# Two-layer graph attention on one core: the second layer's scaled rows made tile by tile inside the projection, with a reference per group of tiles

## The reference

```python
# layer 0, N=4096, F=256, 8 heads of 128
Wh = einsum('nf,hfd->hnd', x, W_heads)
e = s1[:, :, None] + s2[:, None, :]            # s1 = Wh.a1, s2 = Wh.a2
e = where(e > 0, e, 0.2 * e); e = where(adj > 0, e, NEG)
hp = elu(einsum('hnm,hmd->hnd', softmax(e), Wh))
x = layernorm(x + feat @ W_out + b_out)        # feat: 4096 x 1024
# layer 1, 4 heads of 64
xt = einsum('ni,hio->hno', x, W)
e = leaky_relu(src[:, :, None] + dst[:, None, :], 0.2), masked by adj
x = layernorm(x + concat_heads(softmax(e) @ xt))
```

## Time and profile before

| | |
|---|---|
| median of 3 runs | 2834.19 us (2832.05 to 2834.41) |
| the profiled execution | 2831.95 us, span 2830.2 us |
| PE, ACT, DVE, POOL busy | 96%, 72%, 69%, 20% of the span |
| mean granted TensorE clock | 0.987 of full speed |
| stages, start of the first instruction | projection 2066.0, last tile's projection done 2244.2, first attention matmul 2305.9, last 2815.2 us |

### The profile page before, as it was taken

The page is one execution under the profiler, slowest core; times in us unless marked ns, Lnnn a source line. Parts: engine busy times, 40 slices in busy tenths (PEclk is TensorE's granted clock), DMA queues, the critical chain, the costliest instruction groups (busy, mean ns, idle before and its releaser), DMA issues.

```text
span 2830.2 us, 62581 instructions
## 1 busy us (share of the span) xinstructions
PE 2714.5 (96%) x26702; PEld 2350.6 (83%) x26702; DVE 1964.6 (69%) x3078; ACT 2049.7 (72%) x3212; POOL 571.4 (20%) x445
## 2 busy tenths in 40 slices
PE   7889999999999999999999999999999959999997
PEld 3438887888888888888888888888888849999997
DVE  5456678777677776776777767765644468888887
ACT  4447886777777777777787877777722279999996
POOL 0030027233223231422332322310001150000000
PEclk9999999999999999999999999999999979999999
DMA  7985431101110110111110101021134253223330
GB/s 257 396 307 178 154 98 48 30 29 34 29 34 22 40 30 26 37 29 30 33 34 25 38 25 34 22 54 44 25 120 142 86 193 107 93 95 107 111 111 16
DMA packets 189144, 235.19 MB, mean 83 GB/s; under 512 B 13594, under 2 KB 113050, under 8 KB 188860
## 3 DMA queue, kind: packets, MB, share of 16 engines
q1 hardware_dynamic: 188868, 231.20, 25.7%
HBM read 180.49 MB, written 50.66 MB: 82 GB/s over the span
## 4 chain that ended last, share of the span: by engine, by line
PE 73%; DVE 4%; ACT 4%; POOL 2%; issue 1%; ACTq 0%; DVEq 0%; POOLq 0%
PE l_ps L660 56%; PE l_ps L748 11%; PE l_ps L697 4%; ACT l_arena L924 3%; PE l_ps L685 1%; DVE l_arena L1263 1%; DVE l_arena L1262 1%; PE l_ps L717 1%; DVE l_arena L1270 1%; POOL l_arena L370 1%; ACT l_arena L936 1%; POOL l_arena L357 0%; PE l_ps L714 0%; DVE l_arena L1290 0%; DVE l_arena L1251 0%
## 5 line engine op out<-in xcount | busy, mean ns | idle before, releaser
L660 PE MATMUL l_ps<-l_arena 128*128 128x258 f16 x16384 | 1833.3, 273 | 7.1 <-POOL l_arena L346 3.4
L660 PEld LDWEIGHTS l_ps<-l_arena 128*128 128x128 fp8e4 x16384 | 1591.7, 97 | 246.4 <-DVE l_arena L1114 4.3
L855 ACT ACTIVATE l_arena<-l_arena 128x512 fp8e4<-128x512 f32 x2048 | 1281.4, 708 | 89.3 <-PE l_ps L660 89.2
L1113 DVE SCALAR_TENSOR_TENSOR l_arena<-l_arena,l_mask 128x512 uint32<-128x512 uint32 x512 | 468.9, 916 | 407.3 <-ACT l_arena L855 404.6
L748 PE MATMUL l_ps<-l_arena 128*128 128x130 f16 x8192 | 491.6, 222 | 42.9 <-DVE l_arena L1263 40.9
L748 PEld LDWEIGHTS l_ps<-l_arena 128*128 128x128 fp8e4 x8192 | 486.6, 98 | 48.1 <-DVE l_arena L1263 46.5
L1114 DVE TENSOR_TENSOR l_arena<-l_arena,l_mask 128x512 uint32<-128x512 uint32 x512 | 489.9, 957 | 0.0
L924 ACT ACTIVATE l_arena<-l_arena 128x1024 fp8e4<-128x1024 f32 x432 | 453.4, 1141 | 1.2 <-PE l_ps L748 1.2
L339 POOL TENSOR_TENSOR l_arena<-l_arena 128x516 f32<-128x516 f32 x120 | 156.9, 1307 | 1263.4 <-PE l_ps L660 1170.4
L873 ACT COPY l_arena<-l_ps 128x258 f32<-128x258 f32 x256 | 93.7, 369 | 243.5 <-PE l_ps L660 243.5
L1119 DVE SCALAR_TENSOR_TENSOR l_arena<-l_ps,l_arena 128x258 f32<-128x258 f32 x256 | 116.9, 481 | 146.4 <-ACT l_arena L873 146.4
(11 more groups left out here) (142 smaller groups left out, 1246.3 us busy)
## 6 DMA issues: line engine op xcount, KB each, us to landing
l_arena<-in_adj SPq DMA_DIRECT2D x128, 512.0 KB, 7.0
l_arena<-uv SPq DMA_DIRECT2D x128, 260.0 KB, 5.3
l_wh<-l_arena SPq DMA_DIRECT2D x64, 256.0 KB, 9.3
l_arena<-l_srow SPq DMA_DIRECT2D x64, 256.0 KB, 3.3
l_arena<-l_wh SPq DMA_DIRECT2D x64, 256.0 KB, 4.7
feat<-l_arena SPq DMA_DIRECT2D x64, 256.0 KB, 2.2
l_arena<-feat SPq DMA_DIRECT2D x32, 512.0 KB, 3.7
uv<-l_arena SPq DMA_DIRECT2D x8, 1040.0 KB, 4.7
```

What stands on the lines that cost most here:

```text
L660: last = nc.tensor.matmul(sums(t, m), pattern(k, m).bitcast(F8)[:, j, t * P:(t + 1) * P], uv[:, slot(h, order[k]) + j, 2 * m * W1:2 * (m + ...
L855: ins = act.activation(pattern(k, 0).bitcast(F8)[:, j, :], s1b[q][:, :], ACT.Relu, bias=kc[:, h, jt:jt + 1], scale=STEEP, saturate=False)
L1113: dve.scalar_tensor_tensor(c, v, ONE8X4, m, ALU.bitwise_xor, ALU.bitwise_and)
```

## The change

It touches layer 1 only. (a) The scores and rows of a tile come from one matmul pair of 264 columns, two tiles after its projection (`rows_tile`); transposed tiles are kept for two tiles only. (b) Each group c of 4 tiles has its own reference, `kall`: its peak, rounded to a whole multiple of 5 ln 2, so that `eu` and `ev` of a group can be made, scaled and stored (`store_stage`) while later tiles are projected. (c) Once all references are known, `kmax` is the largest; a group's rows then need a factor 2^(5d) or 2^d, d = (kall - kmax)/(5 ln 2), which is exact in f16. `rescales` makes the factors and `rescale(h, k)` multiplies a loaded slice, two instructions of 128x4x130. (d) Each head is rescaled once and stored back (`store_back`): head 0 before and in sweep 0 (slices 0 to 5 ahead of it), head 1 in sweep 0 and behind its `divide2`, head 2 in sweep 1, head 3 in sweep 2. (e) `feat` has two buffers instead of four; slices 0 to 2 of sweep 0's patterns are made in the projection.

The pieces stand in the order of the file: POOL, SP, PE, ACT (its order after the loop last), DVE (in the projection's loop, in the sweeps, at sweep 0's end).

```diff
-            for u in range(PAIRS + 1):
-                if u < PAIRS:
-                    scale2(u)
-                if u > 0:
-                    low2(u - 1)
+                if t >= 9 and t % 4 == 1:
+                    scale2((t - 9) // 4)
+                if t >= 10 and t % 4 == 2:
+                    low2((t - 10) // 4)
+            for c in range(CPB - 2, CPB):
+                scale2(c)
+                low2(c)
...
-                sp.dma_start(fin[t % 4], feat[t * P:(t + 1) * P, :]).then_inc(s_fl[t % 4], 16)
+                sp.dma_start(fin[t % 2], feat[t * P:(t + 1) * P, :]).then_inc(s_fl[t % 2], 16)
...
+            for k in range(CPB - 2):
+                load_uv(0, k)
...
+            store_rows(CPB - 2)
+            for k in range(CPB - 2):
+                store_back(0, k)
+            store_rows(CPB - 1)
+            store_stage(CPB - 2)
+            sp.wait_ge(s_us, 16 * (CPB - 1))
+            load_uv(0, CPB - 2)
+            store_stage(CPB - 1)
...
+            def rows_tile(t):
                 pe.wait_ge(s_xt, t + 1)
+                if t > 0:
+                    pe.wait_ge(s_wc, t)
                 for k in range(KF2):
+                    last = nc.tensor.matmul(pw2, xt2[t % 2][:, k, :], wall2[:, k, :], start=(k == 0),
                                             stop=(k == KF2 - 1))
...
+                    if g < FIRST:
+                        pe.wait_ge(s_res, CPB * g + k + 1)
...
+            def exps(c):
+                act.wait_ge(s_tr2, c + 1)
+                act.activation(by_head(eu2, c), by_head(ta2, c), ACT.Exp).then_inc(s_ex2, 1)
+                act.activation(by_head(ev2, c), by_head(ta2, c), ACT.Exp, scale=SLOPE).then_inc(s_ex2, 1)
...
+            def high_u(c):
+                act.wait_ge(s_tu, c + 1)
+                if c > 0:
+                    act.wait_ge(s_us, 16 * c)
+                act.copy(staged(0), heads(tempu).rearrange("p t h e -> p h t e")).then_inc(s_hu, 1)
...
+            copy_row2(NT - 1)
+            copy_turned(CPB - 1)
+            high_u(CPB - 2)
+            high_v(CPB - 2)
+            compare2(0, 3, range(JC2))
+            exps(CPB - 1)
+            compare2(0, 4, range(JC2))
+            high_u(CPB - 1)
+            high_v(CPB - 1)
+            row_factors()
...
+                ch.link(dve.tensor_scalar(kall[:, c, :], kt, ROUND, ROUND, ALU.add, ALU.subtract))
...
+            def rescale(h, k):
+                q, c = h % 2, SWEEP[h % 2][k]
+                part2 = uv2[:, q, c * JC2 * W4:(c + 1) * JC2 * W4].rearrange("p (t w) -> p t w", t=JC2)
+                dve.wait_ge(s_uv2[q][k], 16 * (h // 2 + 1))
+                dve.tensor_scalar(part2[:, :, 0:2 * V1], part2[:, :, 0:2 * V1], fu.bitcast(F32)[:, c, h:h + 1], None,
+                                  ALU.mult)
+                dve.tensor_scalar(part2[:, :, 2 * V1:], part2[:, :, 2 * V1:], fv.bitcast(F32)[:, c, h:h + 1], None,
+                                  ALU.mult).then_inc(s_res, 1)
...
+                if t >= 8 and t % 4 == 0:
+                    scale_exps((t - 8) // 4)
+                    scale2((t - 8) // 4)
+                if t >= 9 and t % 4 == 1:
+                    low2((t - 9) // 4)
+                if t == 22:
+                    split2(0, 0)
...
+                    if g == 0 and m >= 6:
+                        for n in range(2 * (m - 6), 2 * (m - 5)):
+                            rescale(1, n)
+                    if 0 < g < FIRST - 1 and m >= 4:
+                        for n in range(2 * (m - 4), 2 * (m - 3)):
+                            rescale(g + 1, n)
...
                 evacuate2(g)
                 divide2(g)
+                if g == 0:
+                    for k in range(4, CPB):
+                        rescale(1, k)
```

More of the change, by code:

```diff
@@ L569, in _ @@
                 load_uv(1, k)
+            for k in range(CPB - 2, CPB):
+                store_back(0, k)
             for g in range(G2):
@@ L793, in _ @@
                     turn_x1(t - 1)
[L794 to L795 removed]
+            rows_tile(NT - 2)
+            turn_rows(CPB - 2)
             turn_x1(NT - 1)
[L797 to L807 removed]
+            rows_tile(NT - 1)
+            turn_peaks(CPB - 1)
+            turn_rows(CPB - 1)
+            spread_peaks(CPB - 1)
             for g in range(G2):
@@ L972, in _ @@
                 if t > 1:
-                    copy_scores(t - 2)
+                    copy_row2(t - 2)
+                if t >= 8 and t % 4 == 0:
+                    copy_turned((t - 8) // 4)
+                if t >= 7 and t % 4 == 3:
+                    exps((t - 7) // 4)
+                if t >= 9 and t % 4 == 1:
+                    high_u((t - 9) // 4)
+                    high_v((t - 9) // 4)
+                if t == 16:
+                    compare2(0, 0, [0])
+                elif t == 18:
+                    compare2(0, 0, [1, 2])
+                elif t == 20:
+                    compare2(0, 0, [3])
+                elif t == 22:
+                    compare2(0, 1, [0, 1])
+                elif t == 24:
+                    compare2(0, 1, [2])
+                elif t == 26:
+                    compare2(0, 2, [0, 1])
+                elif t == 28:
+                    compare2(0, 2, [2])
+                elif t == 30:
+                    compare2(0, 2, [3])
                 if t > 0:
```

492 lines of the change are left out of this document (274 added, 218 removed).

## The result

The changed kernel takes **2785.8 us** (median of 4 runs, 2784.4 to 2786.0) against 2833.1 us for the kernel before (4 runs, 2831.1 to 2834.4): a ratio of 0.983, 95% interval 0.982 to 0.985. 2787 had been predicted. The profiled execution took 2785.78 us, its span is 2783.4; the span of before was 2830.2, so 46.8 us are to be found.

What follows compares the result with a forecast made beforehand. TensorE, busy 96% of the span, was taken as the bound. Terms -55.8 + 2.6 + 4.6 + 1 = -47.6 from 2831.95 gave 2784.4, plus 2.2 for the median: 2787 us, range 2775 to 2809.

Steps and rivals of the forecast that it cites:

- The projection: Projection loop on TensorE: 2.6 us longer in all, bounds -1 and +8.
- the pair of score products: In each projection tile: the new pair of 264 columns takes 0.92 us for the old 0.97, 1.6 us less in all.
- what a group adds: In the projection: two transposes and a spreading matmul per group, 0.45 us each for seven groups, 3.2 us.
- rival 4: Projection with two `feat` buffers: loads land too late and the kernel gets slower, 2845 us at 12 us a load; chance 0.04.
- rival 2: Projection lengthens because GpSimd's two large instructions stop VectorE in every group: 21 us, 2808 us; chance 0.12.
- From E to the end of sweep 0: From the last projection's end (E) through attention's first sweep: 44.4 us instead of 100.2, a gain of 55.8 us.
- that of GpSimd: Before sweep 0: GpSimd's low half of group 6 makes VectorE stand once, for 2.1 us.
- Rescaling: VectorE's rescale instructions: 0.29 us each; twelve ahead of sweep 0 at 0.21 after overlap, 2.5 us.
- Sweeps 1 to 3: Attention's next sweeps: 4.6 us late in sweep 1, plus 1 us from VectorE's bunched rescaling in later sweeps.
- Rival 1: Rescale instructions run one element at a time, 0.68 us each: 22 us more, 2809 us; chance 0.12.
- Rival 3: No wait of consequence: sweep 0 ends 39.5 us after the last projection, later sweeps not late, 2776 us; chance 0.10.
- Rival 5: At the projection's end: attention waits for all rows as before, through the last group's DRAM path, 2834 us; chance 0.02.

Runs made afterwards that it cites:

- experiment 9: The kernel before with two buffers for incoming feature tiles instead of four, nothing else: 2830.9 us against 2832.4 (ratio 1.000).
- experiment 2: The changed kernel with GpSimd's `scale2` and `low2` in groups 6 and 7 cut to one tile of four: 2781.2 us.
- the repeat: The changed kernel itself measured again, unaltered, on one chip beside another variant: 2785.8 us.
- Experiment 4: The changed kernel with head 1's rescales spread, three tiles in sweep 0 and five in sweep 1, the next head loaded before storing: 2787.6 us.
- experiment 6: The changed kernel with `row_factors` moved behind slice 5's compares, every head's rescales half a sweep later and next-head loads first: 2780.2 us.

## Why the prediction was right, point by point

- *The projection*: forecast +2.6, measured -0.2. The mis-sized term is the pair of score products. It was costed at 0.92 for 0.97, and took 0.89; and it freed the sixteen products behind it of 0.10 us (3.56 to 3.46), which stood in the earlier trace rows as their own length. An ordinary tile is 0.18 shorter by this (5.43; 5.65 to 5.75 had been named as the sign), 5.8 us in 32. The second mis-sized term is what a group adds, 0.45: its three longer tiles last 5.55, 5.95 and 5.55, so it is 0.76, of which the spreading matmul (L782), taken as two transposes' 0.23, makes 0.52. Seven groups make 5.3 and not 3.2. TensorE has one wait of 0.5 us in the projection, for ScalarE, as before, and one of 0.2 for a `feat` load, where 1 us had been taken (rival 4 is out, see experiment 9); where VectorE was stopped TensorE did not wait (rival 2 is out).
- *From E to the end of sweep 0*: forecast E + 44.4, measured E + 49.8. The places were the ones named: ScalarE idle for the stage's store (2.99 us, not some 5, for 3.10 of its idling fell ahead of that, on a pattern buffer), `row_factors` behind `row_exponents` with ten compares of sweep 0 behind it, TensorE waiting 4.86 us ahead of slice 5. The size was off by 5.4. `row_factors` ran at 30.3 and not 26.5. The step that failed is that of GpSimd: I let VectorE stand for it once, for 2.1 us; it stood three times, and experiment 2, which takes most of that away, has `row_factors` at 26.3. TensorE's first matmul shows the first of them: at 11.4 and not 9 to 10, and at 9.4 in experiment 2. Rescaling (0.265 and not 0.21, twelve times: 0.7) and the store (5.2 and not 4.7) are the smaller parts. The last 1.3 are clock, which the sum had at nothing: the three slices took 12.59, not 11.3. The windows there (us, busy of TensorE, its loads, VectorE, ScalarE, GpSimd; granted clock, DMA share, GB/s):

```profile
2260.00:2276.00 16.00, 15.79 (x271) 15.62 (x268) 14.24 (x14) 7.49 (x8) 8.67 (x6) 1.00 0.47 162
2276.00:2281.00 5.00, 0.35 (x4) 0.35 (x5) 2.77 (x4) 5.00 (x6) 0.00 (x0) 0.89 0.94 276
2281.00:2286.00 5.00, 5.00 (x70) 5.00 (x68) 4.52 (x6) 5.00 (x6) 0.00 (x0) 0.77 0.96 302
```

- *Sweeps 1 to 3*: forecast +5.6 together, measured +4.3. The lateness came in sweep 1, as forecast: it takes 34.3 us where a sweep took 30.55, 3.8 more and not 4.6, and sweeps 2 and 3 add 0.5 and not 1. Sweep 1 ends at E + 84.1 and, in the repeat, at E + 84.0, though sweep 0 ended 1.3 later there, so VectorE holds it. Experiment 4 ties the lateness to the number of rescale instructions in the sweep, 24 here; experiment 6, with 16, takes only a part of it away.
- *Rescaling*: 0.29 had been taken, between 0.29 and 0.43; 0.348 measured. Rival 1 (0.68) is out. The estimate of 0.29 from the Trainium skill, "VectorE: DVE Perf Modes", "The perf-mode tier table (the rule you actually need)", is 0.06 too low; by its 2x the same estimate would be 0.43, so the measured value is the nearer to 4x.
- *The sum*: forecast -47.6, measured -46.2 between the profiled executions and -46.8 between their spans. The terms were off by -2.8, +5.4 and -1.3, and 0.5 came off ahead of the projection: they cancel in part, so it is luck that the total is better than its steps. So is part of the last step: 2.2 were added for the distance between the median and the profiled execution of before, and that distance is 0.04 after. Rival 3 (E + 39.5) is not reached even by the best order tried: it took a start at 9.3 and eight slices at the full clock, and they start at 11.4 and lose 2.0 to the clock. Rival 5 is out.

## What to carry to other kernels

When work moves from behind a boundary to ahead of it, follow the last piece that can't move: here one group's store, its low half and the factors set when the next phase starts, and an engine that waits for them in order should have its ready work in front. A wait at a boundary may be a sum and not an order: compare the engine's busy time between two boundaries with the bound's, and if it is the longer, move work to another period. Before trying a better order, add up what the bound engine itself needs from its first instruction on: here that left sweep 0 one or two microseconds. And look for every large GpSimd instruction that falls beside VectorE's short ones on the chain.
